# Turning exp(q) with DMAs and 32x32 blocks on VectorE instead of transposes on TensorE

## The chip, the cores and the metric

The kernel runs on 1 core of one Trainium2 chip. The metric is the device time of one execution in microseconds (us). Before the change it is 989.16 us, the median of 3 runs (989.14 to 989.24).

## The reference

Two layers of the same kind are applied one after another to x of 8 x 512 x 512 in float32 (batch, sequence, width). Layer 0 has 16 heads of width 32, layer 1 has 8 heads of width 64.

```python
xn = layernorm(x) * w + b
q, k, v = xn @ Wq + bq, xn @ Wk + bk, xn @ Wv + bv      # 512 x 512 each; k and v masked by row
q = softmax(q.reshape(b, t, h, dh), axis=-1)            # within a head
k = softmax(k.reshape(b, t, h, dh), axis=1)             # over the sequence
att = einsum('bnhd,bnhl->bhdl', k, v)
y = einsum('bnhd,bhdl->bnhl', q, att).reshape(b, t, d)
scale, shift = split(silu(emb) @ W_emb + b_emb)
x = x + (silu(layernorm(y) * (1 + scale) + shift) @ W_out + b_out)
```

## The kernel before

There are 16 iterations, one for each layer and batch; iteration i + 8 is layer 1 of batch i. The first and the last of a layer are written out, those between run in a loop on each engine. A batch is 4 tiles of 128 rows; the width is 4 chunks (c or g) of 128 columns. An array x[128, 4, 512] holds the four tiles side by side, one row of a tile per partition.

Products with weights are made at more than single precision: a float32 operand is split into a high part (fp32r) and a low part, and three products per chunk (high by high, high by low, low by high) add up in PSUM. So a projection of one tile is 12 products of 128 x 512 (L368), for K, V, Q and the out projection O alike.

TensorE's order in an iteration i of the middle is written out by hand:

- K projection of the four tiles into `psum_k`, with two transposes of y of iteration i - 1 (`turn_y`, L432) before the last tile and two after it;
- V projection of the four tiles into the two banks of `psum_w`, between them the transposes of the column maxima of k (L527) and one product that spreads them (L532);
- Q projection of the four tiles into `psum_w`;
- k^T v, 16 products (L554), into `psum_k`;
- `out_projection` of iteration i - 1, tile 0, then tile 1;
- in layer 0 `turn_att`: 4 transposes of the attention matrix, into which VectorE has worked the bias of v and the mask of the heads;
- `turn_q(0)`, `turn_q(1)`: 4 transposes of 128 x 128 each (L582) into one of the two banks of `psum_t`, from which ScalarE copies them to `qT` (L1052);
- `out_projection`, tile 2, then `turn_q(2)`, `turn_q(3)`;
- `attend(0)`, `attend(1)`: 4 products each (L592) of `qT` by the attention matrix into `psum_k`;
- `turn_x(i + 1, 0)` and `(i + 1, 1)` (L419, 4 transposes each), `out_projection` tile 3, `turn_x(i + 1, 2)`, `attend(2)`, `turn_x(i + 1, 3)`, `attend(3)`.

`attend(t)` for t of 2 or 3 waits until VectorE has taken tile t - 2 of y out of `psum_k`, and the first K product of the next iteration waits for tile 2 of y.

q goes from TensorE to VectorE (bias added, L856, and the maximum of each head, L859), to GpSimd (maximum subtracted, L1137), and to ScalarE (exponential in place, L1045). The softmax's sum comes from columns of ones beside the attention matrix and is divided out when VectorE makes y from PSUM (L914 a reciprocal, L916 the product). VectorE runs its queue in order: `next_xn` (L659), the attention matrix (L872 to L884), `add_residual` (L790) for tiles 0, 1 and 2 of iteration i - 1, y of tiles 0 and 1, their statistics (L923), `add_residual` of tile 3, y of tiles 2 and 3.

SP issues every DMA: in an iteration it loads x of the next one (L275) and the residual rows (L339), and it stores the finished rows of iteration i - 1 (L343). Iteration 0 (layer 0) and iteration 7 (layer 1) also have a film stage (the embedding's product), whose weights, like those of the next layer, pass through two slots of `raw` by `load_raw` (L270). Wk of layer 1 is split in iteration 7 (L667). In iteration 0 VectorE reduces the masks' rows (`greatest_masks`, L695). In the last iteration there is no next x; there TensorE's order after k^T v is `out_projection` tile 0, `turn_q` 0 to 3, `attend` 0 to 3, `out_projection` tiles 1 and 2, `turn_y` 0 and 1, `out_projection` tile 3. After it come `turn_y` 2 and 3 and the out projection of the last iteration itself.

## Time and profile before

| | |
|---|---|
| median of 3 runs | 989.16 us |
| the profiled execution, first to last instruction | 987.8 us |
| TensorE (PE) busy | 956.6 us, 97% |
| VectorE (DVE) busy | 613.5 us, 62% |
| ScalarE (ACT) busy | 419.1 us, 42% |
| GpSimd (POOL) busy | 284.7 us, 29% |
| mean granted TensorE clock | 0.993 of full speed |
| DMA, mean | 72 GB/s |

The profile gives for the profiled execution its span; the time that the runs measure also has what lies around it. An instruction's length in it runs from its start to its end, and products on TensorE overlap, so what one costs is the distance from its start to the next one's. A group of instructions is listed by line of the kernel, engine, operation and tile, with the idle time before it and what ended that.

### The profile page before, as it was taken

The page shows a single profiled execution, that of the slowest core. Times are in us where ns is not written, and L with a number is a line of the kernel's source. Part 1 is how long each engine was busy: PE and PEld are TensorE (multiplying, and loading weights), DVE is VectorE, ACT ScalarE, POOL GpSimd, SP SyncE. Part 2 cuts the span into 40 slices and gives each one's busy share as a digit, 9 for nine tenths or more (in the row PEclk, how much of TensorE's full clock was granted, in tenths as well). Part 3 has the DMA queues.
Part 4 walks back from the last instruction along what each step waited for, and adds up shares of the span by engine and source line. Part 5 has one row for each costly group of instructions (what it writes and reads, how often), then busy time and mean ns, then how long its engine had stood idle before and what let it go on. Part 6 is the DMA issues. An engine that isn't in the chain of part 4 may idle for free.

```text
span 987.8 us, 14264 instructions
## 1 busy us (share of the span) xinstructions
PE 956.6 (97%) x5066; PEld 798.0 (81%) x5066; DVE 613.5 (62%) x1247; ACT 419.1 (42%) x643; POOL 284.7 (29%) x307
## 2 busy tenths in 40 slices
PE   4989999999999999999999999999999999999987
PEld 3758888888888888886688888888888888888876
DVE  5787655656566555757876656565655556565563
ACT  5536335343443524345463453335335343543522
POOL 2033421314242041422134313142421314242230
PEclk9999999999999999999999999999999999999998
DMA  7543020020302103031460300203020020302002
GB/s 230 221 139 128 1 108 20 5 122 0 127 0 79 49 0 127 0 128 43 128 234 1 114 26 26 104 0 127 0 108 19 16 111 0 127 0 110 18 1 85
DMA packets 19609, 71.21 MB, mean 72 GB/s; under 512 B 3392, under 2 KB 3448, under 8 KB 13440
## 3 DMA queue, kind: packets, MB, share of 16 engines
q1 hardware_dynamic: 19584, 70.88, 19.1%
q8 instruction: 15, 0.25, 0.1%
q14 instruction: 10, 0.08, 0.0%
HBM read 54.10 MB, written 16.78 MB: 72 GB/s over the span
## 4 chain that ended last, share of the span: by engine, by line
PE 91%; DVE 5%; issue 2%; POOL 1%; ACT 0%; POOLq 0%; SPq 0%; DVEq 0%; ACTq 0%
PE psum_w L368 52%; PE psum_k L368 18%; PE psum_k L592 5%; PE psum_k L554 5%; PE psum_t L582 3%; PE psum_t L432 3%; PE psum_t L419 3%; DVE w_low_k L739 1%; PE psum_t L527 1%; PE psum_t L396 1%; POOL q L1137 1%; DVE y L916 0%; DVE y L777 0%; DVE x_in L659 0%; PE psum_k L564 0%
## 5 line engine op out<-in xcount | busy, mean ns | idle before, releaser
L1083 POOL TENSOR_TENSOR xT_low<-xT,xT_high 128x512 fp32r<-128x512 f32 x60 | 77.3, 1288 | 239.6 <-ACT xT_high L980 238.2
L1075 POOL TENSOR_SCALAR x_var<-x_moments 128x4 f32<-128x4 f32 x16 | 3.7, 228 | 373.6 <-DVE x_moments L653 365.6
L1003 ACT ACTIVATE gate<-psum_t,film_shift,film_scale 128x512 f32<-128x512 f32 x64 | 49.7, 776 | 144.1 <-PE psum_t L432 114.0
L368 PE MATMUL psum_k<-w_high_k,xT_high 128*128 128x512 f32 x256 | 105.3, 411 | 0.5 <-DVE y L916 0.5
L368 PE MATMUL psum_w<-w_high_v,xT_high 128*128 128x512 f32 x256 | 103.7, 405 | 0.4 <-DVE emb_parts L823 0.4
L368 PE MATMUL psum_w<-w_high_q,xT_high 128*128 128x512 f32 x256 | 101.2, 395 | 0.0
L368 PE MATMUL psum_k<-w_high_k,xT_low 128*128 128x512 f32 x256 | 101.1, 395 | 0.0
L368 PE MATMUL psum_w<-w_high_v,xT_low 128*128 128x512 f32 x256 | 101.1, 395 | 0.0
L368 PE MATMUL psum_w<-w_low_q,xT_high 128*128 128x512 f32 x256 | 101.1, 395 | 0.0
L368 PE MATMUL psum_w<-w_high_q,xT_low 128*128 128x512 f32 x256 | 101.1, 395 | 0.0
L368 PE MATMUL psum_w<-w_low_v,xT_high 128*128 128x512 f32 x256 | 101.0, 395 | 0.0
L368 PE MATMUL psum_k<-w_low_k,xT_high 128*128 128x512 f32 x256 | 100.9, 394 | 0.0
L368 PE MATMUL psum_w<-w_high_o,gT_high 128*128 128x512 f32 x240 | 98.8, 412 | 0.0
L368 PE MATMUL psum_w<-w_high_o,gT_low 128*128 128x512 f32 x240 | 95.0, 396 | 0.0
L1045 ACT ACTIVATE q<-q 128x512 f32<-128x512 f32 x64 | 40.4, 631 | 128.2 <-POOL q L1137 128.2
L368 PE MATMUL psum_w<-w_low_o,gT_high 128*128 128x512 f32 x240 | 94.4, 393 | 0.0
L790 DVE TENSOR_TENSOR x_res<-x_res,psum_w 128x512 f32<-128x512 f32 x60 | 41.1, 685 | 81.2 <-PE psum_w L368 81.2
L1052 ACT COPY qT<-psum_t 128x512 f32<-128x512 f32 x64 | 34.6, 589 | 132.6 <-PE psum_t L582 132.6
L1021 ACT ACTIVATE v<-psum_w,v_mask 128x512 f32<-128x512 f32 x64 | 44.1, 689 | 95.6 <-PE psum_w L368 95.6
L1115 POOL TENSOR_TENSOR x_res<-x_res,bias_o 128x512 f32<-128x512 f32 x60 | 77.8, 1328 | 5.3 <-DMA x_res<-x_between_layers 5.3
L1137 POOL TENSOR_TENSOR q<-q,q_max 128x512 f32<-128x512 f32 x64 | 71.9, 1151 | 25.5 <-DVE q_max L859 25.5
L856 DVE TENSOR_TENSOR q<-psum_w,bias_q 128x512 f32<-128x512 f32 x64 | 43.7, 683 | 54.7 <-PE psum_w L368 54.7
(135 smaller groups left out, 1985.9 us busy)
## 6 DMA issues: line engine op xcount, KB each, us to landing
x_in<-x_between_layers SPq DMA_DIRECT2D x9, 1024.0 KB, 4.8
x_res<-in_x SPq DMA_DIRECT2D x8, 1024.0 KB, 6.8
x_between_layers<-x_res SPq DMA_DIRECT2D x8, 1024.0 KB, 3.9
x_in<-in_x SPq DMA_DIRECT2D x7, 1024.0 KB, 4.9
x_res<-x_between_layers SPq DMA_DIRECT2D x7, 1024.0 KB, 6.8
out_x<-x_res SPq DMA_DIRECT2D x7, 1024.0 KB, 3.9
raw_weights<-in_L_cond_film_emb_W SPq DMA_DIRECT2D x4, 1024.0 KB, 6.1
raw_weights<-in_L_cond_W_emb SPq DMA_DIRECT2D x4, 1024.0 KB, 5.1
```

What stands on the lines that cost most here:

```text
L368: mm = pe.matmul(bank, lhs[:, c, rows_of_tile], rhs[w][:, c, :], start=(c == 0 and n == 0), stop=(c == CHUNKS - 1 and n == 2))
L554: mm = pe.matmul(att_psum[:, g, 0:VCOLS], k_exp[:, t, g * P:(g + 1) * P], v[:, t, g, :], start=(t == 0), stop=(t == TILES - 1))
L592: mm = pe.matmul(y_psum_of(t)[:, g, 0:BCOLS], qT[:, t, g, :], att_of[layer][:, g, :], start=True, stop=True)
L790: dve.tensor_tensor(x_sum, x_sum, psum_w[:, t % 2, :], ALU.add).then_inc(o_added, 1)
L856: dve.tensor_tensor(q[:, t, :], psum_w[:, t % 2, :], bias_q[:, :], ALU.add)\
L1003: act.activation(gate[:, c % 2, :], psum_t[:, c % 2, :, :].rearrange("p t s -> p (t s)"), ACT.Silu, scale=film_scale[:, cond, c:c + 1].rea ...
L1021: act.activation(v[:, t, :, 0:P], psum_w[:, t % 2, :].rearrange("p (g n) -> p g n", g=CHUNKS), ACT.Copy, scale=v_mask[:, bass.ds(i, 1), t: ...
L1045: act.activation(q[:, t, :], q[:, t, :], ACT.Exp).then_inc(q_exp_ready, 1)
L1052: act.copy(qT[:, t, :, :], psum_t[:, t % 2, :, :]).then_inc(qT_ready, 1)
L1083: pool.tensor_tensor(xT_low[:, c, :], xT[:, c % 2, :], xT_high[:, c, :], ALU.subtract)\
L1115: pool.tensor_tensor(x_biased, x_biased, bias_o[:, :], ALU.add)\
L1137: pool.tensor_tensor(rows_q, rows_q, q_max[:, t, 0:HEADS[layer]].unsqueeze(2) .to_broadcast([P, HEADS[layer], width]), ALU.subtract).then_ ...
```

## The change

After the exponential, q is no longer transposed by TensorE. SP waits for the fourth tile's exponential and issues 16 DMAs from SBUF to SBUF, one for each pair of a source quarter b and a destination quarter `at` of the partitions. Each moves, from 32 partitions to 32 partitions, 4 tiles x 128 columns: 64 KB in pieces of 512 bytes. Then VectorE transposes, for each tile, sixteen 32 x 32 blocks in one instruction (`dve.transpose`), from `q_quads` back into `q`. For this to give chunks as before, the columns of Wq (and of bq) are kept in another order: column c*128 + a*32 + f stands at a*128 + c*32 + f (`by_part`, `as_q_columns`).

The maximum of q is taken over 16 blocks of 32 columns in both layers; in layer 1 a further small operation joins the two blocks of a head. ScalarE's copies of `qT` go. On TensorE `turn_q` goes, `turn_x(i + 1, 0)` and `(i + 1, 1)` stand before `attend(0)`, and in the last iteration the out projections of tiles 1 and 2 stand before `attend(0)`, only that of tile 3 behind `attend(3)`, and `turn_y` 0 and 1 behind that. On SP the dealing stands after the load of the residual rows and before the store; in iterations 0 and 7 some loads of raw weights come behind it. On VectorE the four block transposes stand before `add_residual` of tile 2; in iteration 0 they are behind `greatest_masks(1)`, in iteration 7 behind the split of Wk.

```diff
 GROUP = 256
+QUADS, QUAD = 4, 32
...
         q = sb("q", [P, TILES, DIM])
-        q_max = sb("q_max", [P, TILES, HEADS[0]])
-        qT = sb("qT", [P, TILES, CHUNKS, P])
+        q_max = sb("q_max", [P, TILES, QUADS * CHUNKS])
+        q_head_max = sb("q_head_max", [P, TILES, QUADS * CHUNKS])
+        q_quads = sb("q_quads", [P, TILES, QUADS, P])
+        q_turned = q
...
             return (xT_high, xT_low) if fixed(j, ITERS - 1) else (gT_high, gT_low)
+        def as_q_columns(row):
+            return row.rearrange("p (c a f) -> p a c f", c=CHUNKS, a=QUADS)
+        def by_part(row):
+            return row.rearrange("p (a c f) -> p a c f", a=QUADS, c=CHUNKS)
...
                     at += n
+            def deal_q(i):
+                sp.wait_ge(q_exp_ready, TILES * (i + 1))
+                for at in range(QUADS):
+                    for b in range(QUADS):
+                        sp.dma_start(q_quads[at * QUAD:(at + 1) * QUAD, :, b, :],
+                                     q[b * QUAD:(b + 1) * QUAD, :, at * P:(at + 1) * P]).then_inc(q_dealt, 16)
...
                 if fixed(i, 0):
-                    for n in range(RAW_BEFORE_0, RAW_IN_0):
+                    for n in range(RAW_BEFORE_0, RAW_BEFORE_0 + 4):
...
                 if fixed(i, LAST_0):
-                    for n in range(RAW_IN_0, RAW_IN_LAST_0):
+                    for n in range(RAW_IN_0, RAW_IN_0 + 2):
+                        load_raw(n)
+                deal_q(i)
+                if fixed(i, 0):
+                    for n in range(RAW_BEFORE_0 + 4, RAW_IN_0):
+                        load_raw(n)
+                if fixed(i, LAST_0):
+                    for n in range(RAW_IN_0 + 2, RAW_IN_LAST_0):
...
                 mm.then_inc(film_turned, 1)
+            def bank_free(i, c):
+                if c == 0:
+                    pe.wait_ge(k_shift_rows_ready, i + 1)
+                elif fixed(i, 0):
+                    pe.wait_ge(film_step, 1)
+                elif fixed(i, LAST_0):
+                    pe.wait_ge(film_step, FILM_STEPS + 1)
+                else:
+                    pe.wait_ge(gate_ready, CHUNKS * i)
...
                 elif not fixed(i, 0):
-                    pe.wait_ge(qT_ready, TILES * (i - 1) + c + 3)
+                    bank_free(i - 1, c)
...
                     pe.wait_ge(yn_ready, TILES * (j + 1))
-                if c < 2:
-                    pe.wait_ge(xT_ready, CHUNKS * (min(j + 2, ITERS) if isinstance(j, int) else j + 2) - 1 + c)
+                if c < 2 and fixed(j, ITERS - 1):
+                    bank_free(j, c)
+                elif c < 2:
+                    pe.wait_ge(xT_ready, CHUNKS * (j + 2) - 1 + c)
...
                     mm.then_inc(att_turned, 1)
-                def turn_q(t):
-                    pe.wait_ge(q_exp_ready, TILES * i + t + 1)
-                    if t == 0:
-                        pe.wait_ge(k_shift_rows_ready, i + 1)
-                    elif t == 1:
-                        if with_film:
-                            pe.wait_ge(film_step, FILM_STEPS * layer_film + 1)
-                        elif with_output:
-                            pe.wait_ge(gate_ready, CHUNKS * i)
-                        else:
-                            pe.wait_ge(xT_ready, CHUNKS * i + 4)
-                    else:
-                        pe.wait_ge(qT_ready, TILES * i + t - 1)
-                    for c in range(CHUNKS):
-                        mm = pe.transpose(psum_t[:, t % 2, c, :], q[:, t, c * P:(c + 1) * P], ident[:, :])
-                    mm.then_inc(qT_psum, 1)
                 def attend(t):
-                    pe.wait_ge(qT_ready, TILES * i + t + 1)
+                    pe.wait_ge(q_turned_ready, TILES * i + t + 1)
...
                     for g in range(CHUNKS):
-                        mm = pe.matmul(y_psum_of(t)[:, g, 0:BCOLS], qT[:, t, g, :], att_of[layer][:, g, :],
+                        mm = pe.matmul(y_psum_of(t)[:, g, 0:BCOLS], q_turned[:, g, t * P:(t + 1) * P], att_of[layer][:, g, :],
...
                     film_part(layer_film, 3)
-                if with_output and with_next:
+                if with_output:
...
                     turn_att()
-                turn_q(0)
-                turn_q(1)
-                if with_output and with_next:
+                if with_output:
                     out_projection(out_layer, i - 1, 2)
-                turn_q(2)
-                turn_q(3)
-                if with_next and not with_output:
+                if with_next:
...
                     if with_output:
-                        turn_x(i + 1, 0)
-                        turn_x(i + 1, 1)
...
                 if not with_next:
-                    out_projection(out_layer, i - 1, 1)
-                    out_projection(out_layer, i - 1, 2)
+                    out_projection(out_layer, i - 1, 3)
...
                     turn_y(i, 1)
-                    out_projection(out_layer, i - 1, 3)
...
                 dve.wait_ge(w_high_ready, CHUNKS * (4 * layer + n) + c + 1)
-                dve.tensor_tensor(w_low[m][:, c, :], raw[:, slot * CHUNKS + c, :], w_high[m][:, c, :], ALU.subtract)\
-                   .then_inc(w_low_ready, 1)
+                low, high, loaded = w_low[m][:, c, :], w_high[m][:, c, :], raw[:, slot * CHUNKS + c, :]
+                if m == Q:
+                    low, high, loaded = by_part(low), by_part(high), as_q_columns(loaded)
+                dve.tensor_tensor(low, loaded, high, ALU.subtract).then_inc(w_low_ready, 1)
...
                 dve.tensor_tensor(x_sum, x_sum, psum_w[:, t % 2, :], ALU.add).then_inc(o_added, 1)
+            def turn_q(i):
+                dve.wait_ge(q_dealt, 16 * QUADS * QUADS * (i + 1))
+                for t in range(TILES):
+                    dve.transpose(q_turned[:, :, t * P:(t + 1) * P].rearrange("p c (b j) -> p c b j", b=QUADS),
+                                  q_quads[:, t, :, :].rearrange("p b (c f) -> p c b f", c=CHUNKS))\
+                       .then_inc(q_turned_ready, 1)
...
                     dve.wait_ge(q_psum, TILES * i + t + 1)
-                    dve.tensor_tensor(q[:, t, :], psum_w[:, t % 2, :], bias_q[:, :], ALU.add)\
-                       .then_inc(q_biased, 1)
+                    dve.tensor_tensor(by_part(q[:, t, :]), by_part(psum_w[:, t % 2, :]), as_q_columns(bias_q[:, :]),
+                                      ALU.add).then_inc(q_biased, 1)
                     dve.wait_ge(q_biased, TILES * i + t + 1)
-                    dve.tensor_reduce(q_max[:, t, 0:heads], q[:, t, :].rearrange("p (h e) -> p h e", e=width),
-                                      AX_X, ALU.max).then_inc(q_max_done, 1)
+                    by_block = dve.tensor_reduce(q_max[:, t, :], q[:, t, :].rearrange("p (n f) -> p n f", f=QUAD),
+                                                 AX_X, ALU.max)
+                    if layer == 0:
+                        by_block.then_inc(q_max_done, 1)
+                    else:
+                        by_block.then_inc(q_part_max_done, 1)
+                        dve.wait_ge(q_part_max_done, TILES * (i - BATCHES) + t + 1)
+                        part_max = q_max[:, t, :].rearrange("p (a two c) -> p a two c", two=2, c=CHUNKS)
+                        dve.tensor_tensor(q_head_max[:, t, :].rearrange("p (a two c) -> p a two c", two=2, c=CHUNKS),
+                                          part_max[:, :, 0:1, :].to_broadcast([P, 2, 2, CHUNKS]),
+                                          part_max[:, :, 1:2, :].to_broadcast([P, 2, 2, CHUNKS]), ALU.max)\
+                           .then_inc(q_max_done, 1)
...
                     copy_film_rows(layer_film, 1)
-                if with_output and with_next:
+                if with_output:
...
                     split_weights(1, 0)
+                turn_q(i)
...
                 if not with_next:
-                    add_residual(i - 1, 1)
+                    add_residual(i - 1, 2)
                     normalise_y(i)
-                    add_residual(i - 1, 2)
...
                     split_film(layer_film, 3)
-                for t in range(TILES):
-                    act.wait_ge(qT_psum, TILES * i + t + 1)
-                    act.copy(qT[:, t, :, :], psum_t[:, t % 2, :, :]).then_inc(qT_ready, 1)
-                    if fixed(i, LAST_0) and t == 1:
-                        split_weights(1, 0)
+                if fixed(i, LAST_0):
+                    split_weights(1, 0)
...
                     pool.wait_ge(q_max_done, TILES * i + t + 1)
-                    rows_q = q[:, t, :].rearrange("p (h e) -> p h e", e=width)
-                    pool.tensor_tensor(rows_q, rows_q, q_max[:, t, 0:HEADS[layer]].unsqueeze(2)
-                                       .to_broadcast([P, HEADS[layer], width]), ALU.subtract).then_inc(q_shifted, 1)
+                    blocks_q = q[:, t, :].rearrange("p (n f) -> p n f", f=QUAD)
+                    greatest = (q_max, q_head_max)[layer][:, t, :]
+                    pool.tensor_tensor(blocks_q, blocks_q, greatest.unsqueeze(2)
+                                       .to_broadcast([P, QUADS * CHUNKS, QUAD]), ALU.subtract).then_inc(q_shifted, 1)
```

## Rows read from the trace of the kernel before

**Rows 1.** One iteration: length, busy PE, PEld, DVE, ACT, POOL; PEclk, DMA.

```profile
321.00:378.00 57.00, 57.00 (x309) 48.41 (x308) 33.69 (x70) 23.94 (x36) 17.24 (x18) 1.00 0.12 46
```

**Rows 2.** Groups by line, PE: busy us, mean ns, idle before.

```profile
L582 PE MATMUL psum_t<-ident,q 128*128 128x128 f32 x256 | 34.5, 279 | 0.3 <-ACT qT L1052 0.3
```

**Rows 3.** PE in order of time, layer 0: start us, length us, line, count.

```profile
359.68 0.60 PE L564 MATMUL psum_k<-ident,att 128*128 128x128 f32 x4
360.12 1.04 PE L582 MATMUL psum_t<-ident,q 128*128 128x128 f32 x8
360.91 0.48 PE L368 MATMUL psum_w<-w_high_o,gT_high 128*128 128x512 f32 x1
...
363.77 1.03 PE L582 MATMUL psum_t<-ident,q 128*128 128x128 f32 x8
364.64 1.97 PE L592 MATMUL psum_k<-att,qT 128*128 128x132 f32 x16
366.44 1.04 PE L419 MATMUL psum_t<-ident,x_in 128*128 128x128 f32 x8
367.23 0.48 PE L368 MATMUL psum_w<-w_high_o,gT_high 128*128 128x512 f32 x1
...
372.73 0.49 PE L368 MATMUL psum_k<-w_high_k,xT_high 128*128 128x512 f32 x1
```

**Rows 4.** PE in order of time, layer 1.

```profile
835.32 1.04 PE L582 MATMUL psum_t<-ident,q 128*128 128x128 f32 x8
```

**Rows 5.** ACT in order of time: the last exponential of q, layers 0 and 1.

```profile
353.92 0.63 ACT L1045 ACTIVATE q<-q 128x512 f32<-128x512 f32 x1 [0.56 <-POOL q L1137]
...
829.52 0.63 ACT L1045 ACTIVATE q<-q 128x512 f32<-128x512 f32 x1 [0.55 <-POOL q L1137]
```

**Rows 6.** SP's DMA issues in order of time (length of the issue alone).

```profile
433.36 0.34 SPq L275 DMA_DIRECT2D x_in<-x_between_layers  x1
433.75 0.42 SPq L339 DMA_DIRECT2D x_res<-in_x  x1
...
507.22 0.45 SPq L275 DMA_DIRECT2D x_in<-x_between_layers  x1
507.72 0.43 SPq L339 DMA_DIRECT2D x_res<-in_x  x1
```

**Rows 7.** DMA issues by tensor: KB each, median us to landing.

```profile
raw_weights<-in_L_cond_Wq SPq DMA_DIRECT2D x2, 1024.0 KB, 5.3
...
out_x<-x_in SPq DMA_DIRECT2D x4, 256.0 KB, 2.5
...
masked_in<-in_mask_BxS_ik SPq DMA_DIRECT2D x1, 16.0 KB, 2.7
```

**Rows 8.** DVE in order of time, layer 0: four of a kind, then two y tiles.

```profile
340.31 2.46 DVE L650 BATCH_NORM_STATS2 x_stats<-x_in 128x6 f32<-128x512 f32 x4
...
365.74 0.26 DVE L914 RECIPROCAL q_rsum<-psum_k 128x16 f32<-128x16 f32 x1 [1.09 <-PE psum_k L592]
...
366.64 0.26 DVE L914 RECIPROCAL q_rsum<-psum_k 128x16 f32<-128x16 f32 x1
...
367.54 1.28 DVE L923 BATCH_NORM_STATS2 y_stats<-y 128x6 f32<-128x512 f32 x2
```

**Rows 9.** Groups by line, DVE: the slowest 128x512 form.

```profile
L739 DVE TENSOR_TENSOR w_low_k<-raw_weights,w_high_k 128x512 fp32r<-128x512 f32 x16 | 13.7, 916 | 0.0
```

**Rows 10.** DVE in order of time: ahead of the turns in iterations 0 and 7.

```profile
73.71 2.27 DVE L695 TENSOR_REDUCE mask_top<-x_res 128x4 f32<-128x2048 f32 x1
...
491.08 2.50 DVE L667 TENSOR_TENSOR w_low_k<-raw_weights,w_high_k 128x512 fp32r<-128x512 f32 x4 [0.64 <-ACT w_high_k L958]
```

**Rows 11.** PE in order of time: the first K product of iteration 1.

```profile
81.84 0.50 PE L368 MATMUL psum_k<-w_high_k,xT_high 128*128 128x512 f32 x1 [0.48 <-DVE y L916]
```

**Rows 12.** Windows about PE's wait in the last iteration, columns as in rows 1.

```profile
960.00:965.00 5.00, 0.11 (x1) 0.00 (x0) 5.00 (x5) 0.00 (x0) 4.71 (x4) 0.85 0.00 0
965.00:968.00 3.00, 2.95 (x11) 2.76 (x12) 0.93 (x2) 1.76 (x3) 0.00 (x0) 0.50 0.00 0
```

8 lines of the change are left out of this document (5 added, 3 removed).

## The prediction

> **What bounds the kernel now.** I read the windows first, one per iteration. In an iteration from the middle TensorE is busy for 57.00 of 57 us at a granted clock of 1.00, VectorE for 34, ScalarE for 24 and GpSimd for 17 [rows 1]. So the time is the sum of what TensorE issues, sixteen times over, and two questions decide the change: what leaves TensorE's queue, and whether what takes its place is done when TensorE comes for it.
>
> Then the groups by line. The transposes of q are 256 products with 34.5 us of busy time [rows 2], but busy times overlap, so I price them by starts in the order of time [rows 3]. The first eight start at 360.12 and the next product at 360.91: 0.79 us. The other eight start at 363.77 and the attend at 364.64: 0.87 us. One iteration gives 1.66 us, and I take that for both layers.
>
> **The slack of the new path.** q now goes: last exponential, 16 DMAs on SP, four 32x32-block transposes on VectorE, attend(0). TensorE gets to attend(0) after the out projection of tile 2 and the first eight transposes of x, which move ahead of it. Layer 0: the projection can start at 360.12, takes 363.77 - 360.91 = 2.86, the transposes of x about 0.87: 363.85 [rows 3]. The last exponential ends at 353.92 + 0.63 = 354.55 [rows 5]. That is 9.30 us; less 0.70 for the first VectorE transpose, the DMAs have 8.60 us from the exponential to the last landing. Layer 1 has no transposes of the attention matrix: its out projection of tile 2 can start at 835.32, where its first transposes of q stand [rows 4]; 835.32 + 2.86 + 0.87 = 839.05, less 829.52 + 0.63 = 830.15 [rows 5], less 0.70: 8.20 us.
>
> **The 16 DMAs.** The trace has none from SBUF to SBUF and none of 64 KB in 512 byte pieces. SP issues them one after another: 433.36 to 433.75 is 0.39 us from start to start, 507.22 to 507.72 is 0.50 [rows 6]. I take 0.42, nearer to the first since these issues need no address worked out and stand back to back: 15 x 0.42 = 6.3. From issue to landing 256 KB take 2.5 and 16 KB in 1024 small pieces 2.7 [rows 7]; I take 2.2, as nothing is read from or written to DRAM. Sum 8.5 us. From below: 15 x 0.39 + 1.5 = 7.4. From above, by pieces: if the whole 2.7 us of the 16 KB load were its 64 pieces per engine, one of 16 bytes would take 0.042; the load of 1 MB in pieces of 2 KB, 32 per engine, takes 5.3 us, less 2.5 for latency 0.09 a piece [rows 7]. 512 bytes lie at most halfway, 0.065, and 128 of them per engine make 8.3 + 2.2 = 10.5. At the 2 KB price it would be 11.2 + 2.2 = 13.4.
>
> At 8.5 layer 0 waits for nothing (8.60) and layer 1 waits 0.3 us in each iteration. While VectorE waits for the landing, its residual addition of tile 2 and all of y stand behind; SP's store of the iteration before stands behind the issues, but it waits for a residual addition that is later anyway. Loads of raw weights behind the deal in iterations 0 and 7 come some 6 us later, with more than that in hand for most.
>
> A rule speaks against this. The Trainium skill ("DMA: Bandwidth & Descriptors", Bandwidth, measured) has a 64 KB transfer take 0.95 us and says that under 64 KB one pays mostly overhead; laid end to end, 16 would take 15.2 us by that page. No row here shows how far such small transfers overlap.
>
> **VectorE.** Four transposes of 128x512 per iteration. The nearest rows stream as many elements: four statistics take 2.46, 0.61 from start to start, about 0.69 alone [rows 8]; the dearest form costs 0.92 [rows 9]. I take 0.61, and 0.70 for the first. Where does y then stand? From the landing: turns 2.45, residual 0.65, y of tiles 0 and 1 0.90 each [rows 8], statistics 1.2, residual 0.65, y of tile 2 0.95: 7.7 us. The next K product wants that y. TensorE reaches it 372.73 - 364.64 - 0.79 = 7.30 us after attend(0) starts [rows 3], so at landing + 8.0. It holds, by 0.3 us. At 0.92 per turn it would be missed by about 1.2.
>
> The Trainium skill ("VectorE: DVE Perf Modes", The three transpose paths) gives 311 ns for a 128x128 bf16 transpose in 32x32 blocks. Four of those per tile would be 1.24 us by that page, an estimate, instead of 0.70; no row here shows one.
>
> **What costs nothing.** The maxima over 16 blocks instead of 8 heads and one small operation more per tile in layer 1 (some 0.2 us) lie on VectorE, which idles between tiles of q; GpSimd reaches the last subtraction late anyway, behind its bias work. If that cover went, each would delay the exponential by 0.2 us in layer 1, 1.6 us in all. The reordered weight columns change strides, not counts. ScalarE loses 64 copies that nobody at the bound waits for. One exposure: the earlier transposes of x bring GpSimd's split of x beside VectorE's turns; if the two held each other up, y would lose its 0.3 us and up to 1 us more in layer 1, 7 us in all.
>
> **The ends.** Iteration 0 has no out projections to hide behind. VectorE's 2.27 us mask reduction at 73.71 now stands ahead of the turns [rows 10]: first turn ready at 76.7, y of tile 2 at 75.98 + 6.4 = 82.4 where TensorE, at 81.84, already waited for it [rows 11]. That loses 0.7, and a longer idle stretch (from the transposes of x to the first turn, some 3 us) on TensorE lowers its clock: behind 5 us in which it was busy for 0.11, near the end of the kernel, the next 3 us ran at 0.50 [rows 12]. I book 2.0 lost. Iteration 7: the split of Wk, 2.50 us [rows 10], stands ahead of the turns; gain 0.6. Last iteration: two projections that filled the wait for y (2 x 2.86 = 5.7 us) are now in front of attend, one stays behind it, and none is left to cover ScalarE between the transposes of y. The idle time grows from 5 to about 8 us with the clock at 0.50 after it [rows 12]. Removed transposes against that: 2.0 lost.
>
> **Sum.** Iterations 1 to 6: 6 x 1.66 = 10.0. Iteration 7: 0.6. Iterations 8 to 14: 7 x (1.66 - 0.3) = 9.5. Ends: -4.0. Total 16.1. The profiled execution spans 987.8 us, the runs' median of 989.16 lies 1.4 above; 987.8 - 16.1 + 1.4 = 973.1, so **973 us**.
>
> **Rivals.** With x the time from exponential to landing, the stalls are 6(x - 8.6) + 7(x - 8.2) = 13x - 109, against a gain without stalls of 10.0 + 0.6 + 11.6 - 4.0 = 18.2 (971 us).
> - *As forecast*, x from 7.4 to 9.3: 971 to 983 us. Chance 0.52. For: issues at 0.39 in the rows. Against: no margin.
> - *The deal is late* (the other side): the landing of the last DMA bounds attend(0) in every iteration. It decides from x = 9.8, 0.5 us per issue or 0.06 per piece on an engine. At 10.5, 27.5 of stalls: 998; at 13.4, 65 of stalls: 1036. For: 2048 pieces a time, 32 partitions per DMA. Against: the 0.50 in rows 6 is one of two pairs, and both lie in code that works out addresses between issues. Chance 0.25, of which 0.06 is x between 9.3 and 9.8 with a small gain.
> - *The transfers don't overlap.* Were each to start when the one before has landed, at the 2.2 us taken above, x would be 35 and the time 1317. Against: two loads issued 0.50 us apart [rows 6] take far longer than that to land, so SP doesn't wait for one. Chance 0.02. With the Trainium skill's 0.95 us each ("DMA: Bandwidth & Descriptors", Bandwidth, measured), x is an estimated 17 and the time 1083.
> - *VectorE's turns are slow.* At half the rate of rows 8, 1.22 each, the y chain misses the K product by 1.7 us and attend(0) by 0.5: 13 x 2.2 = 29, 1002 us. At 0.92 [rows 9]: 13 x 1.3 = 17, 990. For: no row shows the form. Against: every 128x512 form in fp32 lies between 0.6 and 0.92. Chance 0.14. The Trainium skill's 311 ns ("VectorE: DVE Perf Modes", The three transpose paths) would land near the first of the two.
> - *Nothing comes of it*: the waits just eat the gain, 987 to 991. Chance 0.07.
>
> **How the numbers follow.** 0.2% is about what a measurement of this kernel can tell from no change. Faster: 0.52, the 0.06 of the late deal, and 0.07 of the slow turns: 0.65. Same 0.07. Slower 0.28. The likeliest case alone spans 967 (both ends free of cost) to 983; the range takes in late deals up to x = 10.5 and slow turns and runs from 966 to 1003, with 0.05 below and 0.15 above.
>
> **What the profile after would show.** L582's group gone, TensorE's products of q, K, V and O unchanged. From the last exponential to the last dealing DMA's landing: 8.5 us. VectorE's new group at 0.61 to 0.69 us with its wait for the DMA before it. TensorE idle before attend(0): none in layer 0, 0.3 us in layer 1. No idle before the first K product. The prediction is wrong if the dealing issues are 0.5 us or more apart, if a turn takes over 0.8 us, or if TensorE's clock falls in the middle iterations.

## The result and the profile after

The changed kernel takes 1053.9 us (median of 4 runs) where the kernel before takes 989.2 us (4 runs beside it): 1.0653 times, 95% interval 1.0632 to 1.0674. It is slower by 65 us. The prediction, 973 us and 966 to 1003, is wrong in sign and in range.

The page of the changed kernel: busy time of each engine, the chain of work that ended last, one group, one issue.

```profile
PE 958.6 (91%) x4810; PEld 794.4 (75%) x4810; DVE 663.6 (63%) x1343; ACT 384.5 (37%) x579; POOL 284.8 (27%) x307
...
PE 51%; SPq 14%; POOL 11%; issue 9%; DVE 8%; DMA 3%; ACT 3%; POOLq 0%; DVEq 0%; ACTq 0%
...
L812 DVE STREAM_TRANSPOSE q<-q_quads 128x512 f32<-128x512 f32 x64 | 39.8, 680 | 81.3 <-DMA q_quads<-q 81.3
...
q_quads<-q SPq DMA_DIRECT2D x256, 64.0 KB, 2.1
```

TensorE executes 256 instructions fewer and is busy for about as long. SP's queue, which did nothing that mattered before, holds 14% of the chain, and VectorE waited 81.3 us for the dealt q. The waits of TensorE by line (us in total, times, longest):

```profile
PE psum_k L616 <- DVE q L812: 59.6, 16, 5.1
PE psum_w L501 <- DMA param_in<-in_L_cond_film_emb_b: 11.2, 1, 11.2
PE psum_t L474 <- DVE y L794: 7.7, 1, 7.7
```

L616 is `attend`, L812 the block transposes, L474 `turn_y` in the last iteration. The first line is new and comes once in each of the 16 iterations. One iteration of layer 0, in order of time (start, length; ScalarE's last exponential, SP's deal, TensorE's first transposes of x, VectorE's turns, attend(0) and (1)); it answers to [rows 3, 5]:

```profile
370.06 0.63 ACT L1083 ACTIVATE q<-q 128x512 f32<-128x512 f32 x1 [0.56 <-POOL q L1172]
370.71 10.34 SPq L307 DMA_DIRECT2D q_quads<-q  x16
...
379.04 1.04 PE L459 MATMUL psum_t<-ident,x_in 128*128 128x128 f32 x8
382.53 2.49 DVE L812 STREAM_TRANSPOSE q<-q_quads 128x512 f32<-128x512 f32 x4 [5.22 <-DMA q_quads<-q]
383.30 3.21 PE L616 MATMUL psum_k<-att,q 128*128 128x132 f32 x16 [3.22 <-DVE q L812]
```

The exponential ends at 370.69, the turns start at 382.53: 11.8 us, not 8.5. The 16 issues take 10.34 us, 0.65 from start to start; the last begins at about 380.4 and lands 2.1 later. The four turns last 2.49, 0.61 each, as forecast. TensorE, done with its transposes of x at about 380.1, waits 3.22. The same in layer 1:

```profile
756.29 0.63 ACT L1083 ACTIVATE q<-q 128x512 f32<-128x512 f32 x1 [0.77 <-POOL q L1172]
756.95 10.27 SPq L307 DMA_DIRECT2D q_quads<-q  x16
...
768.70 2.49 DVE L812 STREAM_TRANSPOSE q<-q_quads 128x512 f32<-128x512 f32 x4 [5.98 <-DMA q_quads<-q]
769.47 3.65 PE L616 MATMUL psum_k<-att,q 128*128 128x132 f32 x16 [3.85 <-DVE q L812]
```

Attend's 16 products lasted 1.97 us before [rows 3]; here 3.21 and 3.65. Windows about that wait, columns as in [rows 1]:

```profile
381.00:383.00 2.00, 0.00 (x0) 0.00 (x0) 0.47 (x1) 1.40 (x3) 1.76 (x2) 1.00 0.32 66
383.00:385.00 2.00, 1.70 (x11) 1.70 (x12) 2.00 (x5) 0.00 (x0) 0.78 (x1) 0.76 0.00 0
385.00:387.00 2.00, 2.00 (x9) 1.91 (x9) 1.88 (x6) 0.00 (x0) 0.00 (x0) 0.50 0.00 0
387.00:390.00 3.00, 3.00 (x15) 2.43 (x15) 1.91 (x4) 0.00 (x0) 0.00 (x0) 0.92 0.00 0
```

In these windows the granted clock is still full while TensorE stands idle, and falls to 0.50, its lower level of 1.2 GHz, once it works again: the iteration pays for its wait a second time. Over iterations 1 to 6 the mean granted clock is 0.97.

**Where the 65 us lie.** The first K product of an iteration marks its start:

```profile
84.08 0.49 PE L397 MATMUL psum_k<-w_high_k,xT_high 128*128 128x512 f32 x1 [0.55 <-DVE y L952]
...
453.87 0.48 PE L397 MATMUL psum_k<-w_high_k,xT_high 128*128 128x512 f32 x1
...
529.06 0.47 PE L397 MATMUL psum_k<-w_high_k,xT_high 128*128 128x512 f32 x1
...
963.23 0.48 PE L397 MATMUL psum_k<-w_high_k,xT_high 128*128 128x512 f32 x1
```

The starts of iterations 1, 7, 8 and 15. Before, they were at 81.84 [rows 11], 430.87, 501.53 and 905.61. The last column is that of an experiment below, "two queues, ends in order", worked out the same way (all in us, the differences against before). The first stretch is the least sure: that kernel took 80.7 us for it and "the tail filled", which is the same up to there, 83.5.

| stretch | before | after | difference | forecast | two queues |
|---|---|---|---|---|---|
| up to iteration 1 | 81.8 | 84.1 | +2.2 | +2.0 | -1.1 |
| iterations 1 to 6 | 349.0 | 369.8 | +20.8 | -10.0 | -10.3 |
| iteration 7 | 70.7 | 75.2 | +4.5 | -0.6 | -0.6 |
| iterations 8 to 14 | 404.1 | 434.2 | +30.1 | -9.5 | -12.1 |
| iteration 15, to the end | 82.2 | 89.6 | +7.4 | +2.0 | +3.7 |
| span | 987.8 | 1052.8 | +65.0 | -16.1 | -20.5 |

### The profile page after: what moved, and what is told of

It is laid out like the page before. It is cut to its first block, busy times and chain, and to the rows that moved or that the text cites. A ratio compares the mean times of both kernels' runs of the same rounds, so it can differ in the third digit from the quotient of the medians.

```text
span 1052.8 us, 14012 instructions
## 1 busy us (share of the span) xinstructions
PE 958.6 (91%) x4810; PEld 794.4 (75%) x4810; DVE 663.6 (63%) x1343; ACT 384.5 (37%) x579; POOL 284.8 (27%) x307
## 4 chain that ended last, share of the span: by engine, by line
PE 51%; SPq 14%; POOL 11%; issue 9%; DVE 8%; DMA 3%; ACT 3%; POOLq 0%; DVEq 0%; ACTq 0%
PE psum_w L397 22%; PE psum_k L397 17%; SPq L307 14%; PE psum_k L616 8%; POOL q L1172 5%; POOL x_res L1150 5%; DMA q_quads<-q 3%; PE psum_t L474 3%; DVE k_exp L868 2%; PE psum_t L459 1%; DVE x_stats L665 1%; DVE q L812 1%; ACT q L1083 1%; ACT k_shift_rows L1071 1%; PE psum_t L569 1%
## 5 line engine op out<-in xcount | busy, mean ns | idle before, releaser
L616 PE MATMUL psum_k<-att,q 128*128 128x132 f32 x512 | 87.7, 335 | 59.8 <-DVE q L812 59.6
L1014 ACT ACTIVATE xT<-psum_t,params 128x512 f32<-128x512 f32 x64 | 49.7, 776 | 238.5 <-PE psum_t L459 238.5
L616 PEld LDWEIGHTS psum_k<-att,q 128*128 128x128 f32 x512 | 80.6, 241 | 64.0 <-DVE q L812 63.6
L397 PE MATMUL psum_w<-w_high_o,gT_high 128*128 128x512 f32 x240 | 101.7, 424 | 0.0
L812 DVE STREAM_TRANSPOSE q<-q_quads 128x512 f32<-128x512 f32 x64 | 39.8, 680 | 81.3 <-DMA q_quads<-q 81.3
```

Source lines behind the costliest of these rows:

```text
L397: mm = pe.matmul(bank, lhs[:, c, rows_of_tile], rhs[w][:, c, :], start=(c == 0 and n == 0), stop=(c == CHUNKS - 1 and n == 2))
L616: mm = pe.matmul(y_psum_of(t)[:, g, 0:BCOLS], q_turned[:, g, t * P:(t + 1) * P], att_of[layer][:, g, :], start=True, stop=True)
L812: dve.transpose(q_turned[:, :, t * P:(t + 1) * P].rearrange("p c (b j) -> p c b j", b=QUADS), q_quads[:, t, :, :].rearrange("p b (c f) -> ...
L1014: act.activation(xT[:, c % 2, :], psum_t[:, c % 2, :, :].rearrange("p t s -> p (t s)"), ACT.Identity, scale=params[:, layer, LN_SCALE + c: ...
```

## The experiments

The theory after the result: the price is that of one DMA issue on SP, whatever it carries, and it makes attend(0) late; the clock adds to it. The rivals: the pieces or the SBUF source set the price; the small transfers load the DMA engines or SBUF for all others; VectorE or TensorE's new order costs the time by itself.

**Two queues.** ScalarE issues half of the deal.

```diff
 # deal_q on SP
-                    for b in range(QUADS):
+                    for b in range(0, 2):
 # ScalarE, behind its exponentials
+                act.wait_ge(q_exp_ready, TILES * (i + 1))
+                for at in range(QUADS):
+                    for b in range(2, QUADS):
+                        act.dma_start(q_quads[at * QUAD:(at + 1) * QUAD, :, b, :],
+                                      q[b * QUAD:(b + 1) * QUAD, :, at * P:(at + 1) * P]).then_inc(q_dealt, 16)
```

> The 16 dealing DMAs are shared: SP issues those with source quarter b of 0 and 1, ScalarE those with b of 2 and 3, after its own last exponential. Theory A (the rate of issue on one queue, 0.65 us each, makes the deal late; the engines that move the data are half idle): 8 issues take 7 x 0.65 = 4.5 us, landing 2.1 us later, 6.7 us after the exponential, inside the 8.1 to 8.6 us that TensorE leaves. TensorE's idle time before attend(0) is gone in the iterations of the middle, the attends go back to some 0.11 us per product, and the kernel comes to 971 to 976 us. Theory B (the engines are held up by 512-byte pieces from 32 partitions, and SP's issues only back up behind them): two queues share the same engines, each issue takes about 1.3 us, the last landing stays near 11.8 us after the exponential, and the time stays near 1054 us.

Measured 978.6 us, 0.9884 times before (0.9867 to 0.9900). Faster than both kernels with the same bytes, pieces and transfers. In order of time:

```profile
354.43 0.63 ACT L1083 ACTIVATE q<-q 128x512 f32<-128x512 f32 x1 [0.56 <-POOL q L1177]
...
355.08 5.14 SPq L307 DMA_DIRECT2D q_quads<-q  x8
...
355.09 5.47 ACTq L1089 DMA_DIRECT2D q_quads<-q  x8
...
362.27 2.49 DVE L812 STREAM_TRANSPOSE q<-q_quads 128x512 f32<-128x512 f32 x4 [0.60 <-DMA q_quads<-q]
...
364.27 1.97 PE L616 MATMUL psum_k<-att,q 128*128 128x132 f32 x16
```

The queues issue their eight 0.65 and 0.69 us apart, side by side: they don't share the cost. The turns start 7.2 us behind the exponential, attend(0) waits for nothing and lasts its old 1.97. TensorE's waits show what is still lost: one of 9.4 us in iteration 0 (3.2 in the changed kernel), where ScalarE's issues stand ahead of the split of film weights that TensorE needs.

**Four wide transfers.** The same 1 MB in the same 2048 pieces, in 4 issues.

```diff
-                for at in range(QUADS):
-                    for b in range(QUADS):
-                        sp.dma_start(q_quads[at * QUAD:(at + 1) * QUAD, :, b, :],
-                                     q[b * QUAD:(b + 1) * QUAD, :, at * P:(at + 1) * P]).then_inc(q_dealt, 16)
+                for b in range(QUADS):
+                    sp.dma_start(q_quads[:, :, b, :], q[:, :, b * P:(b + 1) * P]).then_inc(q_dealt, 16)
```

> In place of 16 DMAs of 32 partitions, SP issues 4 of 128 partitions, with the same 2048 pieces of 512 bytes in all, each quarter of the columns copied to its block without a change of partition: the deal itself is left out, q isn't turned rightly. Theory A, with a price per DMA: last issue 3 x 0.65 = 2 us after the first, landing by 5 us: no wait in the middle, 971 to 976 us. Theory A, with a price per piece or per partition at issue: an issue takes up to 2.6 us and nothing changes, 1054 us. Theory B: 2048 pieces take as long as before, near 1054 us.

Measured 969.5 us, 0.9794 (0.9777 to 0.9810). Four issues take 2.72 us and the stall in the middle is gone. The quarters stay on their partitions here, so q isn't turned; the time shows what the change is worth where the deal is in time. An issue for 128 partitions is no cheaper than the deal's: 0.68 from start to start.

**A quarter of the bytes and of the pieces, one long piece, and a source in DRAM.** Each edits the two tensors of the 16 DMAs and leaves their number; none deals the whole of q to its place.

```diff
 # one tile each
-                        sp.dma_start(q_quads[at * QUAD:(at + 1) * QUAD, :, b, :],
-                                     q[b * QUAD:(b + 1) * QUAD, :, at * P:(at + 1) * P]).then_inc(q_dealt, 16)
+                        sp.dma_start(q_quads[at * QUAD:(at + 1) * QUAD, b, b, :],
+                                     q[b * QUAD:(b + 1) * QUAD, b, at * P:(at + 1) * P]).then_inc(q_dealt, 16)
 # one piece of 2 KB
+                        sp.dma_start(q_quads[at * QUAD:(at + 1) * QUAD, b, :, :].rearrange("p b n -> p (b n)"),
+                                     q[b * QUAD:(b + 1) * QUAD, at, :]).then_inc(q_dealt, 16)
 # from x in DRAM
+                                     rows(source[0], 0)[b * QUAD:(b + 1) * QUAD, :, at * P:(at + 1) * P])
```

> The same 16 DMAs between the same partitions, but each moves one tile instead of four: 32 pieces of 512 bytes instead of 128, 16 KB instead of 64 (three quarters of q aren't dealt; the space is filled once at the start by GpSimd). A price per DMA: issues stay 0.65 us apart, the landing near 11.8 us after the exponential, time within 5 us of 1054. A price per piece, at issue or on the engines: issues come 0.2 to 0.4 us apart, no wait, 971 to 980 us.

> The 16 DMAs keep their number, bytes and partitions, from SBUF to SBUF, but each partition moves one piece of 2 KB instead of four of 512 bytes (q isn't dealt rightly). If an issue costs by the shape of its pattern, 0.39 to 0.45 us and 970 to 980 us. If it costs 0.65 us for any DMA from SBUF to SBUF, landing by 12 us and 1048 to 1056 us.

> The 16 DMAs keep their number, sizes, pieces of 512 bytes and destinations, but read x in DRAM instead of q in SBUF (the turned data isn't q). If an issue costs 0.65 us because source and destination are both in SBUF, issues fall to 0.39 to 0.45 us as for the kernel's own loads, the last landing comes 8 to 9 us after the exponential and the time is 970 to 980 us. If it costs 0.65 us for its shape (32 partitions by 4 pieces) whatever the source, nothing changes: 1050 to 1058 us.

One run each: 1042.1, 1053.2 and 1064.1 us. SP's issues in the middle of each, in that order:

```profile
366.00 10.04 SPq L307 DMA_DIRECT2D q_quads<-q  x16
```

```profile
369.36 10.04 SPq L307 DMA_DIRECT2D q_quads<-q  x16
```

```profile
374.39 10.27 SPq L307 DMA_DIRECT2D q_quads<-in_x  x16
```

Sixteen issues take 10 us in all three, and they land 1.8, 2.0 and 2.4 us after their issue. So the price of an issue for 32 partitions is not set by its bytes, its pieces or its source; what these change is the landing, and with it the wait at L616 (49.5, 55.2 and 62.5 us in total).

**Does the deal disturb others?** The kernel before, with the 16 DMAs into a tile that nobody reads.

```diff
+            def deal_q(i):
+                sp.wait_ge(q_exp_ready, TILES * (i + 1))
+                for at in range(4):
+                    for b in range(4):
+                        sp.dma_start(q_quads[at * 32:(at + 1) * 32, :, b, :],
+                                     q[b * 32:(b + 1) * 32, :, at * P:(at + 1) * P]).then_inc(q_dealt, 16)
```

> The kernel before with the 16 dealing DMAs added in each iteration, into a tile that nobody reads; TensorE still turns q. If the loss lies only in who waits for the deal, the time stays within 2 us of 989. The rival: 16 more transfers of 64 KB take SBUF or queue time from the others (256 of them, 10.3 us of SP each iteration); then it is 992 us or more, with longer waits for x or the residual.

Measured 989.5 us, ratio 1.000 (0.9989 to 1.0010). 256 transfers a run cost nothing where nobody waits for them. Contention is out; what is left is the wait and what it does to the clock.

**Filling the wait.** Unused transposes keep TensorE busy until q is turned.

```diff
                     turn_x(i + 1, 1)
+                    if with_output:
+                        for n in range((30, 38)[layer]):
+                            pe.transpose(psum_k[:, 3, 0:P], ident[:, :], ident[:, :])
                 attend(0)
```

> The changed kernel, with 30 (layer 0) and 38 (layer 1) needless 128x128 transposes of the identity on TensorE between the transposes of x and attend(0), into a free bank: they fill 3 to 4 us in which it waited, in iterations 1 to 7 and 8 to 14. Theory C (part of the loss is TensorE's clock, which falls to half behind each wait): the clock stays at 1.00, attend(0), attend(1) and the out projection behind them lose 1.6 us per iteration, 14 x 1.6 = 22: 1030 to 1034 us. Rival (the slow stretch comes from something else, as contention with VectorE's turns or the split of x): nothing is gained, 1052 to 1058 us.

Measured 1033.9 us, 1.0441 (1.0423 to 1.0458), 20 us less than the changed kernel, with work added. Its window over the filled wait and attend, and TensorE's L638, the filling:

```profile
375.00:385.00 10.00, 10.00 (x78) 9.23 (x76) 7.51 (x14) 3.74 (x6) 3.03 (x3) 1.00 0.14 42
```

```profile
374.32 3.44 PE L638 MATMUL psum_k<-ident 128*128 128x128 f32 x30
```

The clock stays at 1.00, in this window and as the mean over iterations 1 to 6 and 8 to 14. An iteration of layer 0 is 61.6 us long in the changed kernel, 60.0 with the filling, and 58.2 before: 1.6 us are the clock, and the 1.8 that stay are the bare stall less the gain, 3.2 - 1.66 = 1.5, and 0.3 more. By the starts of the K products the 14 filled iterations are 22.9 us shorter in all, and the two ends, which the edit doesn't touch, 2.4 longer (the last with a mean granted clock of 0.89 instead of 0.94). So of the 65 us some 20 to 23 are the clock behind the stalls.

**A wait does not always cost the clock.** In iterations 3 and 10 of the kernel with a quarter of the bytes it did not fall, though TensorE waited as long there as in their neighbours. Iteration 2, then 3: attend(0) and (1), and a window behind their start.

```profile
196.51 2.90 PE L616 MATMUL psum_k<-att,q 128*128 128x132 f32 x16 [2.69 <-DVE q L812]
198.00:201.00 3.00, 3.00 (x12) 2.63 (x12) 2.93 (x7) 0.00 (x0) 0.00 (x0) 0.50 0.00 0
...
257.54 2.07 PE L616 MATMUL psum_k<-att,q 128*128 128x132 f32 x16 [2.66 <-DVE q L812]
259.00:262.00 3.00, 3.00 (x18) 2.53 (x17) 2.93 (x7) 0.00 (x0) 0.00 (x0) 1.00 0.00 0
```

Iteration 3 lasts 59.4 us where iteration 2 lasts 61.0, and iteration 10, with a wait of 3.32, lasts 59.6 where iteration 11 with the same wait lasts 61.3. That gives the price of the clock once more, 1.6 to 1.7 us. Why it held in these two is not shown.

**Twelve issues, the diagonal on GpSimd.** The four quarters that stay on their partitions are copied by GpSimd.

```diff
                     for b in range(QUADS):
+                        if at == b:
+                            continue
 # GpSimd, ahead of split_x
+                for at in range(QUADS):
+                    quarter = slice(at * QUAD, (at + 1) * QUAD)
+                    pool.tensor_copy(q_quads[quarter, :, at, :], q[quarter, :, at * P:(at + 1) * P]).then_inc(q_copied, 1)
```

> One queue, 12 DMAs: the four blocks that stay on their partitions are copied by GpSimd instead, which is idle then. Theory A: the last landing comes 0.1 + 11 x 0.65 + 2.1 = 9.3 us after the exponential instead of 11.9, so TensorE waits 0.7 us in layer 0 and 1.1 in layer 1, too short a wait for the clock to fall: 6 x 0.7 + 7 x 1.1 = 12 above the 969.5 us of the kernel that doesn't wait, 980 to 984 us, faster than before the change. If the clock falls behind waits of 1 us too, some 20 us more: 1000 us or above.

Measured 995.6 us, 1.0048 (1.0032 to 1.0064): a miss, by 12 us. Most of the middle behaves: 12 issues in 7.71 us, the turns 9.2 behind the exponential, a wait of 0.56 us in layer 0 and 1.29 in layer 1 with the clock still at 1.00, iterations of 57.3 and 57.5 us. The prediction's formula gives 982 at x = 9.2. The profiled execution, 997.4 us, lies 15 over it: 8 in iterations 0, 7 and 15 (+3.5, +1.8 and +6.3 against before, where the prediction had +3.4 for the three), and 7 in the middle, where the waits sum to 13.9 us instead of 10.6 and iteration 9 alone is 2.7 longer than its neighbours. There the issues take 8.75 us instead of 7.71, TensorE waits 2.32, about 1 more than beside it, and the clock falls, which is the other 1.6:

```profile
610.68 3.06 PE L619 MATMUL psum_k<-att,q 128*128 128x132 f32 x16 [2.32 <-DVE q L816]
613.00:615.00 2.00, 2.00 (x8) 1.71 (x7) 1.93 (x5) 0.00 (x0) 0.00 (x0) 0.50 0.00 0
```

The changed kernel has the same place, with a deal of 11.50 us and a wait of 5.08 in iteration 9. What makes single issues longer is not shown. GpSimd's copies aren't free either: VectorE's last step on the attention matrix beside them, which reads SBUF alone, takes 1.57 us instead of 1.14; the step before it, which reads PSUM too, keeps its 1.12.

**Two queues, ends in order.** As the first, but in iteration 0 ScalarE issues behind its split of film weights, and VectorE takes the mask reduction behind the turns.

```diff
                 if with_film:
                     split_film(layer_film, 3)
+                act.wait_ge(q_exp_ready, TILES * (i + 1))
...
-                if fixed(i, 0):
-                    greatest_masks(1)
                 if fixed(i, LAST_0):
                     split_weights(1, 0)
                 turn_q(i)
+                if fixed(i, 0):
+                    greatest_masks(1)
```

> As the two queues, but ScalarE issues its half behind the fourth film split in iterations 0 and 7, and in iteration 0 VectorE reduces the masks behind its turns instead of ahead of them. Theory A: the middle stays as it was (no wait before attend(0)); the wait of 9.4 us before TensorE's fourth film part in iteration 0 goes back to 3.2, which gives 6 us, and the turns of iteration 0 some 1 to 2 us more: 970 to 973 us against 978.6. Rival (the 9 us that the two queues lie above the kernel with four wide DMAs are lost in the middle, by a landing that is still late or by ScalarE's time): 976 to 979 us.

Measured 970.6 us (968.2 to 972.3), 0.9799 (0.9784 to 0.9815): faster than both kernels, and the whole computation. Its stretches stand in the table above. In the middle it gives what the forecast booked for the removed transposes (10.3 and 12.1 us for 10.0 and 11.6). It changes the order at two places at once, so the 8 us that it gains on the first two-queue kernel are not divided between them.

**The tail filled.** The one before, and in the last iteration the out projection of tile 2 back behind the attends, and 70 unused transposes ahead of `turn_y`.

```diff
-                if with_output:
+                if with_output and with_next:
                     out_projection(out_layer, i - 1, 2)
...
                 if not with_next:
-                    out_projection(out_layer, i - 1, 3)
+                    out_projection(out_layer, i - 1, 2)
+                    bank_free(i, 1)
+                    for n in range(70):
+                        pe.transpose(psum_t[:, 1, 0, :], ident[:, :], ident[:, :])
                     turn_y(i, 0)
                     turn_y(i, 1)
+                    out_projection(out_layer, i - 1, 3)
```

> The kernel with two queues and their ends put in order (970.6 us), and the last iteration changed: the out projection of tile 2 goes back behind the attends, and 70 unused transposes keep TensorE busy while it would wait for y. If the tail's loss is TensorE standing idle and then running at half clock, this gives back 2 to 5 us: 966 to 968. The rival: VectorE and ScalarE set the tail's length whatever TensorE does; then it stays within 1 us of 970.6.

Measured 969.9 us (968.4 to 971.0), the same as without. The windows about `turn_y` and behind it, first of the kernel without the filling, then with:

```profile
944.00:950.00 6.00, 3.75 (x16) 2.71 (x16) 2.69 (x4) 3.91 (x7) 0.50 (x1) 0.68 0.00 0
950.00:954.00 4.00, 3.67 (x11) 2.95 (x12) 1.46 (x3) 1.38 (x3) 0.00 (x0) 0.66 0.64 262
```

```profile
944.00:950.00 6.00, 6.00 (x56) 5.96 (x55) 4.43 (x4) 0.54 (x1) 4.14 (x3) 1.00 0.01 3
950.00:954.00 4.00, 3.69 (x21) 2.97 (x20) 1.98 (x3) 3.03 (x6) 0.00 (x0) 1.00 0.00 0
```

In these windows the clock stays up, and the last iteration is 84.6 us long instead of 85.8: 1.2 us for it, and the runs vary by more. The test isn't clean, though: without the out projection of tile 2 ahead of it, attend(0) waits 2.86 us instead of 0.20, and the clock falls there instead (a mean of 0.57 from 934 to 938 us, 1.00 without the filling). So filling the wait for y gains nothing measurable, as the rival said; how much of the tail is the clock stays open.

**What sets the price of an issue.** Unused DMAs in the kernel before, each on a line of its own: first in one order, then in another.

```diff
 # first order
+                sp.dma_start(probe_b[:, 0, :], x_rows[:, 0, :]).then_inc(probed, 16)
+                sp.dma_start(probe_b[:, 1, :], q[:, 0, :]).then_inc(probed, 16)
+                sp.dma_start(probe_b[0:32, 2, :], x_rows[0:32, 0, :]).then_inc(probed, 16)
+                sp.dma_start(probe_b[32:64, 2, :], q[32:64, 0, :]).then_inc(probed, 16)
+                sp.dma_start(probe_b[64:96, 2, :], q[0:32, 1, :]).then_inc(probed, 16)
+                sp.dma_start(probe_b[96:128, 2:4, 0:P], x_rows[0:32, 0:2, 0:P]).then_inc(probed, 16)
+                sp.dma_start(probe_b[96:128, 2:4, P:2 * P], q[0:32, 0:2, 0:P]).then_inc(probed, 16)
+                sp.dma_start(probe_b[0:96, 3, :], x_rows[0:96, 1, :]).then_inc(probed, 16)
...
 # second order
+                sp.dma_start(probe_b[0:32, 2, :], x_rows[0:32, 0, :]).then_inc(probed, 16)
+                sp.dma_start(probe_b[:, 0, :], x_rows[:, 0, :]).then_inc(probed, 16)
+                sp.dma_start(probe_b[:, 1, :], x_rows[:, 1, :]).then_inc(probed, 16)
+                sp.dma_start(probe_b[32:64, 2, :], q[32:64, 0, :]).then_inc(probed, 16)
+                sp.dma_start(probe_b[64:96, 2, :], q[0:32, 1, :]).then_inc(probed, 16)
+                sp.dma_start(probe_b[96:128, 2, :], x_rows[0:32, 0, :]).then_inc(probed, 16)
+                sp.dma_start(probe_b[:, 3, :], q[:, 0, :]).then_inc(probed, 16)
```

> The kernel before with eight unused DMAs per iteration, each on a line of its own, that differ in one thing at a time: source in DRAM or SBUF, 128, 96 or 32 partitions, same or other partitions, one piece per row or two. My theory: an issue that stands directly behind another costs SP 0.60 to 0.65 us whatever its form, and the 0.39 us of the kernel's own x loads belongs to something about them that I have not found. The rival: the form sets it, and at least one form (the whole-tile load from DRAM, that the kernel itself uses) costs 0.30 to 0.45 us while those from SBUF or of 32 partitions cost 0.6.

> In the probe before, the first issue of each row (a tile of 256 KB from DRAM) cost 0.34 us and every later one 0.53 to 0.64, but place and form went together there. Now the row begins with 32 partitions from DRAM, then come two whole tiles from DRAM, then 32 partitions from SBUF twice, 32 from DRAM, and a whole tile from SBUF. If the place sets the price (only the first of a row is cheap), the first costs 0.34 and the two whole tiles 0.55 or more. If the form sets it (128 whole rows from DRAM is the cheap one), the two whole tiles cost 0.34 to 0.40 and the first about 0.59.

989.1 and 989.9 us, one run each. SP's issues in order of time (start, length of the issue), the first order and then the second:

```profile
353.74 0.34 SPq L349 DMA_DIRECT2D probe_b<-in_x  x1
354.13 0.53 SPq L350 DMA_DIRECT2D probe_b<-q  x1
354.70 0.59 SPq L351 DMA_DIRECT2D probe_b<-in_x  x1
355.33 0.56 SPq L352 DMA_DIRECT2D probe_b<-q  x1
355.93 0.61 SPq L353 DMA_DIRECT2D probe_b<-q  x1
356.58 0.58 SPq L354 DMA_DIRECT2D probe_b<-in_x  x1
357.20 0.64 SPq L355 DMA_DIRECT2D probe_b<-q  x1
357.89 0.58 SPq L356 DMA_DIRECT2D probe_b<-in_x  x1
```

```profile
353.37 0.34 SPq L349 DMA_DIRECT2D probe_b<-in_x  x1
353.76 0.42 SPq L350 DMA_DIRECT2D probe_b<-in_x  x1
354.22 0.43 SPq L351 DMA_DIRECT2D probe_b<-in_x  x1
354.69 0.54 SPq L352 DMA_DIRECT2D probe_b<-q  x1
355.27 0.59 SPq L353 DMA_DIRECT2D probe_b<-q  x1
355.91 0.58 SPq L354 DMA_DIRECT2D probe_b<-in_x  x1
356.54 0.52 SPq L355 DMA_DIRECT2D probe_b<-q  x1
```

Both count. At the head of a row the load of 32 partitions costs 0.34, the same load farther back 0.58 or 0.59. Behind the head, a whole tile from DRAM costs 0.42 or 0.43, a whole tile from SBUF 0.52 to 0.54, and 32 partitions of either, one piece each, 0.54 to 0.61. It isn't the 32 that counts: 96 partitions from DRAM cost 0.58 as well. Two pieces a partition cost 0.58 from DRAM and 0.64 from SBUF. My theory, one price of 0.60 to 0.65 for all, falls, and so does each of the two pure ones. The issues that the prediction had rows for are the cheap form, a tile of 128 partitions from DRAM; the deal's are among the dear ones. In the changed kernel the deal's first issue is no cheaper than the others (the shortest of 256 is 0.585), so the place in the row doesn't explain all there either.

## Why the prediction was wrong

**The failed step** is "I take 0.42, nearer to the first since these issues need no address worked out and stand back to back: 15 x 0.42 = 6.3". It is 15 x 0.65 = 9.75. The other half of x, the landing, was 2.1 for 2.2 taken. With these x is 11.8 and not 8.5. The bounds didn't hold it either. The upper one, 10.5, was built from pieces, and the pieces don't set the issue (with a quarter of them it is still 0.63); the 0.50 for the issue came from the same form of load as the 0.39. The form differed from the rows in partitions and in source. Against a whole tile from DRAM each of the two alone makes the issue dearer (0.58 and 0.53 for 0.42), but they don't add up: for 32 partitions the source makes no difference (0.64 from either, start to start).

**The rival "the deal is late" is what happened**, with its place, its sign and its condition (0.5 us per issue). Its formula at 11.8 gives 13 x 11.8 - 109 = 44 us of stalls and 971 + 44 = 1015. The kernel with the filled wait, 1033.9, lies 18 to 19 above that. The stall is in iterations 0, 7 and 15 as well, which the formula left out: they are 11.6 us over their forecast in that kernel (its K products start at 84.8, 444.9, 518.6 and 941.0, its span is 1032.2). The 13 others are 6.6 us over: layer 1's slack was 0.3 too large (2.1 us), layer 0's iterations are the 0.3 longer that was named above (1.8), and iterations 8 and 9 are 0.9 and 0.6 longer than the rest. About 1 us is not accounted for.

**The second miss, on top,** is that a stall of 3 to 4 us costs TensorE its clock: some 20 us by the filled wait. The prediction had named it as a sign of being wrong, and had the row for it [rows 12], but priced it for the ends alone and not for the rival, so that its 1015 could not reach 1054. In the middle iterations of the twelve issues the clock did not fall behind waits of 0.56, 1.29 and 1.73 us, and fell behind 2.32; in the changed kernel it fell in or right behind each wait of 3.2 to 5.1. But with a quarter of the bytes it fell behind 2.69 and not behind 2.66, nor behind 3.32 in iteration 10, so the length of the wait alone doesn't decide it. The Trainium skill ("TensorE: Matmul & The Clock Gate", HAM oscillation) describes a loop in which a wait for a DMA in each pass lowers the clock, and the cost is paid in every pass; the windows behind the wait agree (0.50 from 385 to 387 us), for every pass of the changed kernel and for 11 of 13 with a quarter of the bytes.

**What held.** The removed transposes are worth 1.66 us an iteration: with the deal in time, iterations 1 to 6 gain 10.3 us (10.0 forecast), iteration 7 0.6 (0.6). The slack of layer 0: 8.60 forecast; landing at 11.8 makes 3.2 of wait, measured 3.22. That of layer 1, 8.20, was 0.3 too large (11.8 - 3.85 = 7.9). Turns at 0.61, and no wait before the first K product in the middle (its only one, 0.55 us, is at iteration 1). With the deal in time and the ends as they were, the four wide transfers take 969.5 us, where the forecast without stalls was 971; that leaves little room for a cost of the reordered maxima or the copies that went. In the last iteration the wait before `turn_y` grew from 4.95 us (the stretch of [rows 12]) to 7.7, where about 8 was forecast. The +2.2 of the first stretch against +2.0 is partly luck: the turns there waited 0.62 us for the deal, where the forecast had the mask reduction hold them up, and the stretch varies by more than that between executions.

**The other rivals.** "The transfers don't overlap": x is 11.8 and not 35, out. "VectorE's turns are slow": 0.61, out. Its price at 0.92 a turn had a slip: 4 x 0.31 less the 0.3 in hand is 0.9 and not 1.3 an iteration, which makes 985 and not 990. "Nothing comes of it": out. By the Trainium skill's 0.95 us for a transfer of 64 KB ("DMA: Bandwidth & Descriptors", Bandwidth, measured), 16 laid end to end are an estimated 15.2 us; the trace doesn't bear that out, the whole deal landed within 11.8. Its remark that issuing from several engines saves only the sequencer's time, "which is usually small relative to the DMA itself" (the same page, Issuing engines are not separate DMA queues), reads the other way round in this kernel: that time, 10.3 us, is most of the 11.8 that attend(0) waits for in every iteration, and halving it by a second queue brings 75 us (1053.9 to 978.6).

**Still open:** why an issue for less than a whole tile, or one from SBUF, is dearer; why single issues are longer in some iterations; what besides its length decides whether a wait costs TensorE its clock.

## What to carry to other kernels

A row of DMAs that somebody waits for took, here, its count times the price of an issue, plus one landing; bytes and pieces came after that. Price the issue from a DMA of the same form (partitions, source, pieces a partition, place in a row); if the trace has none, the nearest form is no bound, and the time from which the rival decides says how much it may be off. Where the count can't be lowered, deal the issues to two queues, but look at what stands behind them on the second. And where a rival is a wait of TensorE in every iteration, price the clock behind it too: here it was 1.6 us on top of waits of 3.2 to 3.9.

## What the runs showed of the hardware

- SP took 0.63 to 0.65 us from one issue to the next for SBUF to SBUF transfers between groups of 32 partitions, with 16 or 64 KB, with pieces of 512 bytes or 2 KB, and from DRAM too. SP and ScalarE issued side by side at 0.65 and 0.69. Four transfers of 128 partitions with 512-byte pieces were 0.68 apart.
- An fp32 transpose of 32x32 blocks, 128x512, takes 0.68 us, 0.61 from start to start: as long as the residual addition of a tile (0.68 to 0.69).
- In iterations 1 to 6 and 8 to 14 of the changed kernel the granted clock fell to 0.50 in or right behind each of TensorE's waits of 3.2 to 5.1 us, at a price of about 1.6 us each; with a quarter of the bytes it held at 1.00 behind two of 13 waits, 2.66 and 3.32 us.
- While SP dealt, the DMA engines fell idle between two transfers. Their busy share in the changed kernel, 372 to 380 us in 40 slices of 0.2 us (tenths):

```profile
DMA  7706804922941860770591392195087068049229
```

A burst about every three slices, one for each issue: the issues filled the time, not the transfers.
